# Decoder layer on one core: the filter network's operands first in the DMA queues, its matmuls ahead of the first projections, and the first right taps behind the first filter's sums

## What is computed

```python
res = u @ w_in.T + b_in                          # 768 channels: x0, x1, v
res = _depthwise_conv3(res.transpose(0, 2, 1), conv_w, conv_b)
x, v = res.reshape(B, 3, D, L)[:, :-1], res.reshape(B, 3, D, L)[:, -1]
pe = jnp.sin(t * bands * FREQ)                   # (1024, 33), a constant
h = jnp.sin(FREQ * (pe @ w1.T + b1)) @ w2.T + b2 # the filter network, (1024, 2*256)
h = h * exp(-exp(filt_decay) * t) + filt_bias
for n in range(2):                               # irfft(rfft(v) * rfft(h[n]))[..., :L]
    v = circular_free_convolution(v, h[n]) * x[:, n]
```

## Time and profile before

| | |
|---|---|
| three runs | 823.0, 826.23, 826.8 us, median 826.23 |
| profiled execution | 830.26 us, span 828.1 us from the first to the last instruction |
| busy in the span | PE 702.4 us (85%), DVE 643.4 (78%), ACT 382.0 (46%), POOL 372.0 (45%) |
| mean granted TensorE clock | 0.951 |

### The profile page before, as it was taken

One profiled execution on the slowest core, in us unless ns is written; L12 is line 12 of the kernel. 1 busy time (PEld: TensorE's weight loads), 2 busy tenths in 40 slices (PEclk: granted clock), 3 DMA queues, 4 the chain that ended last, 5 costly groups with the idle time before them and its releaser, 6 DMA issues. The chain is left out here.

```text
span 828.1 us, 12514 instructions
## 1 busy us (share of the span) xinstructions
PE 702.4 (85%) x4398; PEld 507.9 (61%) x4414; DVE 643.4 (78%) x1194; ACT 382.0 (46%) x701; POOL 372.0 (45%) x519
## 2 busy tenths in 40 slices
PE   3889998977989779987798988689999947888893
PEld 1378756866658566576676854477777732555552
DVE  2798778899888998789988751458888826899982
ACT  4432264301473113822126245656666634777773
POOL 0733425653148531485416512707423123476776
PEclk9999999989999899998999999789999996999998
DMA  8250055230052720527410557400000000000012
GB/s 292 80 102 1 0 136 119 51 51 0 7 95 55 179 21 1 102 51 144 73 52 25 137 143 258 149 2 2 2 2 2 2 0 2 1 27 27 33 45 76
DMA packets 37049, 52.79 MB, mean 64 GB/s; under 512 B 4761, under 2 KB 31386, under 8 KB 36732
## 3 DMA queue, kind: packets, MB, share of 16 engines
q0 software_dynamic: 7680, 16.77, 12.7%
q1 hardware_dynamic: 28604, 33.92, 12.3%
q10 hardware_dynamic: 704, 1.32, 0.6%
HBM read 31.04 MB, written 8.39 MB: 48 GB/s over the span
## 5 line engine op out<-in xcount | busy, mean ns | idle before, releaser
L644 ACT ACTIVATE yb<-banks 128x256 f32<-128x256 f32 x64 | 24.4, 385 | 230.2 <-PE banks L407 171.4
L398 PE MATMUL banks<-inv_m,spec_y 128*128 128x256 f32 x384 | 87.6, 381 | 8.0 <-POOL spec_y L765 8.0
L431 PE MATMUL banks<-xt_in,w_in 128*128 128x512 f32 x192 | 86.1, 604 | 3.3 <-DMA xt_in<-in_x_t 3.3
L398 PEld LDWEIGHTS banks<-inv_m,spec_y 128*128 128x128 f32 x384 | 72.3, 190 | 20.7 <-POOL spec_y L765 11.2
L355 PE MATMUL banks<-z_cplx,fwd_m 128*128 128x256 f32 x240 | 73.0, 386 | 10.5 <-DVE prod L989 7.5
L764 POOL TENSOR_TENSOR spec_y<-prod 128x256 f32<-128x256 f32 x64 | 49.2, 769 | 64.1 <-DVE prod L989 63.0
L356 PE MATMUL banks<-z_cplx,fwd_m 128*128 128x256 f32 x240 | 72.3, 383 | 0.0
L431 PEld LDWEIGHTS banks<-xt_in,w_in 128*128 128x128 f32 x192 | 37.0, 194 | 48.6 <-issue 48.4
L369 PE MATMUL banks<-z,fwd_m 128*128 128x256 f32 x168 | 46.0, 436 | 21.0 <-DVE sums_c L936 16.1
L355 PEld LDWEIGHTS banks<-z_cplx,fwd_m 128*128 128x128 f32 x240 | 45.5, 192 | 19.4 <-issue 9.7
L988 DVE TENSOR_TENSOR prod<-banks,spec_h 128x512 f32<-128x512 f32 x64 | 44.0, 687 | 15.5 <-POOL spec_y L765 6.5
(11 more groups left out here) (237 smaller groups left out, 1725.7 us busy)
## 6 DMA issues: line engine op xcount, KB each, us to landing
xt_in<-in_x_t SPq DMA_DIRECT2D x4, 1024.0 KB, 6.6
x_tok<-in_x SPq DMA_DIRECT2D x8, 512.0 KB, 4.3
x_tok<-in_b_out POOLq DMA_DIRECT2D x8, 512.0 KB, 13.2
x_scratch<-x_tok SPq DMA_DIRECT2D x8, 512.0 KB, 2.9
x<-x_scratch SPq DMA_DIRECT2D x8, 512.0 KB, 8.8
v_t<-left POOLq DMA_DIRECT2D x8, 511.5 KB, 5.5
x_t<-left POOLq DMA_DIRECT2D x8, 511.5 KB, 5.0
out<-x SPq DMA_DIRECT2D x7, 512.0 KB, 2.9
```

The source lines that it names most:

```text
L398: last = mm(bank[:, odd * 2 * P:(odd + 1) * 2 * P], spec_y[:, j + odd, part * D + h * P:part * D + (h + 1) * P], inv_m[:, o:o + 2 * P], st ...
L431: last = mm(proj_pair(b, t)[:, c * 512:(c + 1) * 512], w_in[:, k, TILES[t] * P:(TILES[t] + 1) * P], xt_in[:, k, c * 512:(c + 1) * 512], st ...
```

## The change

SP issues `w2` and `b2` directly behind `pe_t` and `w1`, and then `xt_in`. The two loads of `b1` go to ACT's queue, behind `filt_decay` and `neg_t`, with a semaphore of their own, so that PE's first matmuls wait for two transfers and not for four. ACT issues `filt_bias` ahead of `w_in`, and the three small loads of the convolution behind it. PE runs the eight tiles of L470 ahead of the projections of `v`. DVE runs the eight decay products and its two bias adds ahead of the six small operations, and the right taps of `v` behind `filter_sums(0)`, ahead of those of `x0`.

```diff
@@ -213,7 +213,7 @@
         I_0, I_2, I_1, I_5 = range(4)
         QUARTERS = (0, 2, 1, 3)
 
-        ld_net = sem("ld_net"); ld_w2 = sem("ld_w2"); ld_rate = sem("ld_rate"); ld_bias = sem("ld_bias")
+        ld_net = sem("ld_net"); ld_b1 = sem("ld_b1"); ld_w2 = sem("ld_w2"); ld_rate = sem("ld_rate"); ld_bias = sem("ld_bias")
         ld_w_in = sem("ld_w_in"); ld_conv = sem("ld_conv"); ld_ident = sem("ld_ident"); ld_w_out = sem("ld_w_out")
         ld_fwd = sem("ld_fwd"); ld_inv = sem("ld_inv")
         ld_xt = sem("ld_xt"); ld_xtok = [sem(f"ld_xtok{g}") for g in range(2)]; st_x1 = sem("st_x1")
@@ -288,13 +288,11 @@
                         sp.wait_ge(st_x1, 16 * (i + 1))
                         load_group(b + 1, g)
 
-            for dst, src in ((pe_t, d["c_pe"]), (w1, d["w1_t"]), (b1[0:HID], d["b1"]), (b1[HID:P], d["b1"])):
+            for dst, src in ((pe_t, d["c_pe"]), (w1, d["w1_t"])):
                 sp.dma_start(dst, src).then_inc(ld_net, 16)
-            load_xt(0)
             for dst, src in ((w2[0:HID], d["w2_t"]), (w2[HID:HID + 1], d["b2"])):
                 sp.dma_start(dst, src).then_inc(ld_w2, 16)
-            for dst, src in ((b_in[:], d["b_in"]), (conv_w[:], d["conv_w"]), (conv_b[:], d["conv_b"])):
-                sp.dma_start(dst, src).then_inc(ld_conv, 16)
+            load_xt(0)
             sp.dma_start(fwd_m[:], d["c_fwd"].rearrange("p (k c) -> p k c", c=P)).then_inc(ld_fwd, 16)
             sp.dma_start(ident[:], d["c_ident"]).then_inc(ld_ident, 16)
             sp.dma_start(inv_m[:], d["c_inv"]).then_inc(ld_inv, 16)
@@ -453,14 +451,10 @@
                     last.then_inc(out_mm, 1)
 
 
-            pe.wait_ge(ld_net, 16 * 4)
+            pe.wait_ge(ld_net, 16 * 2)
             for c in range(2):
                 last = mm(IB[0][c * HID:(c + 1) * HID, :], w1, pe_t[:, c * 512:(c + 1) * 512], start=True, stop=True)
             last.then_inc(hid_mm, 1)
-            pe.wait_ge(ld_w_in, 16)
-            pe.wait_ge(ld_xt, 16)
-            for t in range(T_X1):
-                project_tile(0, t)
             pe.wait_ge(ld_w2, 16 * 2)
             for i in range(L // P):
                 if i % 4 == 0:
@@ -468,6 +462,10 @@
                 if i >= 4:
                     pe.wait_ge(h_used, i - 3)
                 mm(IB[i % 4][:, :], hid[:, i * P:(i + 1) * P], w2, start=True, stop=True).then_inc(h_mm, 1)
+            pe.wait_ge(ld_w_in, 16)
+            pe.wait_ge(ld_xt, 16)
+            for t in range(T_X1):
+                project_tile(0, t)
             for t in range(T_X0, T_ALL):
                 pe.wait_ge(h_used, 6 + 2 * (t - T_X0))
                 project_tile(0, t)
@@ -583,8 +581,12 @@
 
             act.dma_start(decay_rate, d["filt_decay"].broadcast_to([P, 2 * D])).then_inc(ld_rate, 16)
             act.dma_start(neg_t, d["c_negt"]).then_inc(ld_rate, 16)
+            for dst in (b1[0:HID], b1[HID:P]):
+                act.dma_start(dst, d["b1"]).then_inc(ld_b1, 16)
+            act.dma_start(filt_bias, d["filt_bias"].broadcast_to([P, 2 * D])).then_inc(ld_bias, 16)
             act.dma_start(w_in[:], d["w_in_t"].rearrange("(t p) n -> p t n", p=P)).then_inc(ld_w_in, 16)
-            act.dma_start(filt_bias, d["filt_bias"].broadcast_to([P, 2 * D])).then_inc(ld_bias, 16)
+            for dst, src in ((b_in[:], d["b_in"]), (conv_w[:], d["conv_w"]), (conv_b[:], d["conv_b"])):
+                act.dma_start(dst, src).then_inc(ld_conv, 16)
             act.wait_ge(ld_rate, 16 * 2)
             fn(decay_rate, decay_rate, ACT.Exp).then_inc(act_seq, 1)
             act.wait_ge(act_seq, 1)
@@ -875,7 +877,7 @@
 
             nc.vector.memset(hid[HID:HID + 1, :], 1.0).then_inc(hid_ready, 1)
 
-            dve.wait_ge(ld_net, 16 * 4)
+            dve.wait_ge(ld_b1, 16 * 2)
             dve.wait_ge(hid_mm, 1)
             ts(arg, IB[0], b1, FREQ, ALU.add, ALU.mult).then_inc(vec_seq, 1)
             dve.wait_ge(vec_seq, seq.tick())
@@ -888,6 +890,15 @@
                 dve.wait_ge(vec_seq, seq.tick())
             ts(arg, arg, PI_CLAMP, -PI_CLAMP, ALU.min, ALU.max).then_inc(sin_arg, 1)
 
+            for i in range(L // P):
+                dve.wait_ge(h_mm, i + 1)
+                dve.wait_ge(decay_ready, i + 1)
+                tt(h_time[:, i, :], IB[i % 4][:, :], decay[:, i, :], ALU.mult).then_inc(h_used, 1)
+            dve.wait_ge(ld_bias, 16)
+            for i in range(POOL_BIASED, L // P):
+                dve.wait_ge(h_used, i + 1)
+                tt(h_time[:, i, :], h_time[:, i, :], filt_bias, ALU.add).then_inc(taps_last, 1)
+
             dve.wait_ge(ld_conv, 16 * 3)
             tt(b_mid[:], conv_w[:, :, 2], b_in[:], ALU.mult).then_inc(bias_seq, 1)
             dve.wait_ge(bias_seq, 1)
@@ -898,15 +909,6 @@
             tt(b_end[:], conv_b[:], prod[:, 0, 0:6], ALU.add).then_inc(bias_seq, 1)
             tt(b_mid[:], b_mid[:], prod[:, 0, 0:6], ALU.add).then_inc(bias_seq, 1)
             tt(b_left[:], b_in[:], conv_w[:, :, 0], ALU.mult).then_inc(bias_seq, 1)
-
-            for i in range(L // P):
-                dve.wait_ge(h_mm, i + 1)
-                dve.wait_ge(decay_ready, i + 1)
-                tt(h_time[:, i, :], IB[i % 4][:, :], decay[:, i, :], ALU.mult).then_inc(h_used, 1)
-            dve.wait_ge(ld_bias, 16)
-            for i in range(POOL_BIASED, L // P):
-                dve.wait_ge(h_used, i + 1)
-                tt(h_time[:, i, :], h_time[:, i, :], filt_bias, ALU.add).then_inc(taps_last, 1)
 
             def quarter_sums(x0, x1, x2, x2_copy, x3_copy, s, evacuated=None):
 
@@ -1066,12 +1068,10 @@
                                        ALU.mult, ALU.add, accum_out=row_sum[:, g, t:t + 1])
                         last.then_inc(out_used, 1)
 
-            for t in range(T_V, T_X1):
-                right_tap(0, t)
             dve.wait_ge(taps_ready, POOL_BIASED)
             dve.wait_ge(taps_last, L // P - POOL_BIASED)
             filter_sums(0)
-            for t in range(T_X0, T_ALL):
+            for t in (*range(T_V, T_X1), *range(T_X0, T_ALL)):
                 right_tap(0, t)
             filter_sums(1)
             turned_sums(0)
```

## The result

Nine runs of the changed kernel have a median of 830.18 us (829.47 to 832.04), nine of the kernel before 826.25 (823.0 to 829.04): ratio 1.005, 95% interval 1.003 to 1.0069. The forecast was 828.0 us and no change. The measured 3.9 us lie just inside the 4.1 us that the prediction called no change, the time lies inside its range, and the shift is twice the 1.8 us that the sum had. The profiled execution took 830.65 us with a span of 828.7 us. The span before was 828.1 us, but of an execution 4 us above its kernel's median; so the two spans can't be set against each other, and what moved is read from the start of the program.

The account below looks back on a forecast made before the run. Start of TensorE's step q = 2 taken as the bound: 42.9 + 6.9 + 1.75 + 1.75 = 53.3 us against 51.46, so 1.8 us added to the median 826.23 gives 828.0 us; range 822.5 to 832.0.

Parts of the forecast that it names:

- The rule that decides: TensorE's prologue: the change is worth what it moves the start of step q = 2 (51.46 us), passed on one for one.
- A: Whole prologue: right tap's place, small operations, GpSimd's pass and slow restart eat the earlier taps; 828.0 us, 825 to 831; chance 0.56.
- B: TensorE before q = 0: clock does not fall in the gap, ScalarE's evacuation binds; 825.9 us, no change; chance 0.26.
- C: Prologue: neither clock nor first work slow, VectorE's sums take 9.6 us; q = 2 at 45.3, 820.0 us; chance 0.07.
- D: Sine's argument: b1 lands late, with xt_in at 14.87 us; 5.2 us more, 833.2 us; chance 0.11.
- The right tap is late next: TensorE's step q = 0 waits for v's right tap, now behind VectorE's sums: 42.9 us against 40.32.
- T: End of VectorE's first right tap of v, when step q = 0 can start; forecast 42.9 us.
- GpSimd's pass and the small operations: VectorE's first filter: small operations 1.0, sums 9.6, GpSimd's first pass of real sums 3.8 us; end at 41.7.
- The evacuation chain: From right tap via GpSimd's left-tap DMA to ScalarE's first evacuation: 6.5 us, ending 49.5, hidden by the slow clock.
- The issues on ScalarE: ScalarE's start: five added load issues, 0.6 us each, end at 5.6 us; the sine can start at 13.9.
- The eight products: TensorE's second network product: 7.03 us plus 2.2 as first long work, from 14.7 to 23.9 us.
- The slow restart: TensorE's step q = 0 after a 4.9 us gap runs at a lowered clock: 2.5 us more, bounds 0 and 2.8.

Follow-up runs that it names:

- e4: Changed kernel with eight unused TensorE products of 128 rows added between the network's first and second product; 827.85 us.
- e2: Changed kernel with the two right taps of v put back ahead of the first filter's sums; 828.16 us.
- e3: Changed kernel with the three small loads (b_in, conv_w, conv_b) issued by SyncE behind xt_in instead of by ScalarE; 829.19 us.
- e5: Changed kernel with eight unused TensorE products of 65 rows added between the network's first and second product; +9.5 us against the kernel before (one run).
- e8: e7 with the operands of the network's eight second products padded with zeros from 65 to 128 rows; 823.34 us.
- e10: e8 with VectorE's six small operations put back ahead of the decay products; 817.81 us.
- e7: Changed kernel with e2's and e3's edits together, no products added; 824.54 us.

## Why the prediction was nearly right, and where its size was off

The direction and the place were right: the gain is lost between the taps and q = 2, behind the right tap. That the time came out inside the range and as no change is in part luck: the shift of q = 2 was 5.2 us and not 1.8, two terms of the sum were too small by 6.5 us together, two too large by 3.9, and only 3.9 us of the shift show in the time.

- **The rule that decides** held: the taps arrive earlier, and the gain is lost before q = 2, which moved to 56.65 us and passed on (+5.08 at the first inverse, +3.9 in time). The time is A's, 830.2 in 825 to 831, but not all of A came: three of its four causes did, the slow restart did not. In that one point B was right, the clock stayed up in the gap and ScalarE's evacuation bound TensorE; yet the gap was 2.40 us, not the 4.9 that B was about, and e4's of 5.32 did cost. C and D were not: `b1` landed by 7.51 us, not late.
- **The right tap is late next** held. T was forecast at 42.9 us and was 47.9; e2 shows that the place of the taps costs 3.4 us by itself.
- **GpSimd's pass and the small operations** held closely: from 31.00 + 1.28 = 32.3 us to 46.64 is 14.4 us, and the sum had 1.0 + 9.6 + 3.8 = 14.4. The split was different: part of GpSimd's pass fell on the small operations.
- **The evacuation chain** held: from the tap's end 47.9 to 54.17 + 0.59 = 54.76 us, 6.9 us against 6.5, and it bound TensorE by 0.47 us.
- **The issues on ScalarE** were too cheap. I priced five at 0.6 us each and had the table load at 5.6 us; it came at 7.32, and the sine at 15.59 instead of 13.9. e3 measured the three small ones at 3.1 us in place of my 1.8. The activation did follow its table load after 1.29 us (15.59 - 14.30). So the 830.7 us that the prediction names for a drain behind each load (828.0 and 2.8 are 830.8) is near the measured time by accident.
- **The eight products** are the term that was sized most wrongly. "They last 7.03 us in a running engine", and for the first long work "2.2 us more", so 9.2; they took 13.99. I took the cost of the first long work from the projections, which have 128 rows. In this chain the first long work has 65. With 65 rows the rise did not come in 27.7 us (e5), with 128 it did (e4, e8). That is 4.8 us of the chain. With the 1.7 of the issues, less 1.4 because the last bias adds were shorter (1.28 us instead of 2.64), it makes 5.1, against the 5.0 us by which T was off.
- **The slow restart** ahead of q = 0 was forecast at 2.5 us and did not come: the projections ended 7.7 us later than I had them, so the gap was 2.40 and not 4.9 us, and L367 took its 4.55 us. This error had the other sign. Where the gap is 5.32 us (e4) the cost is 2.3 us, about as priced.

The errors: +4.8 and +1.7, -1.4 (bias adds), -2.5 (restart), +0.5 (evacuation): +3.1, against 56.65 - 53.3 = 3.35 us measured. The rest are starts of a tenth or two each, as the 0.18 us from the tap's end to L367. The low end of the range, 822.5, is 0.7 us below what its three terms give (2.2 + 0.5 + 2.1 = 4.8 below 828.0).

What stays open: why the difference in time departs from the prologue's by up to 1.6 us, and whether the clock's falls further on explain all of it; no run isolated that. In the two profiled executions the prologue differs by 5.1 us and the span by only 0.6: behind the prologue the execution before was 4.5 us slower, and its mean granted clock was 0.951 against 0.959.

## What to carry to other kernels

When a chain is moved ahead, list every wait that its last link's consumer has, and look which of them stands behind the moved work in its own engine's order: here the network was early, and TensorE waited for a right tap that had nothing to do with it. A transfer's issue is work of the engine that issues it: on an engine that is on the chain, even the issue of a 3 KB load took 0.7 to 0.8 us and that of a 9 KB load 1.5. And the work at the start of a program should use as many rows as there are, because here its own speed and that of what followed depended on it; zero rows did as well (e8, e10).

## What the runs showed of the hardware that was not expected

- Products that use 65 of the 128 rows did not raise TensorE's clock from rest: 27.7 us of them ran at 1.7 us each (e5, one execution), and the eight of the changed kernel, e2, e3 and e7 took 13.99 us every time. Padded with zero rows, the same eight took 8.84 and 9.98 us (e8, e10). Once it is up, 65 rows keep it up for at least their 7.03 us.
- The clock column does not show this. For the stretch after in which each product took twice its time, and for one at full speed, it reads 1.00 alike:

```profile
16.30:23.30 7.00, 6.93 (x8) 1.00 1.03 374
...
34.00:46.00 12.00, 11.67 (x28) 1.00 0.00 1
```

  Eight records in 6.93 us are 0.87 us each, two to a product, which is twice the 0.43 of the earlier trace rows. That this is the lower level, 1.2 GHz, is read from the durations; at the start of a program I would believe them and not the column.
- VectorE's operations of 6 columns with both operands in SBUF waited up to 1.0 us for GpSimd, much as those of 512 columns do (1.76 us for what takes 0.68). The Trainium skill, SBUF — State Buffer, section Who interferes with whom, says that a VectorE instruction with two SBUF inputs contends with a GpSimd instruction that reads SBUF, and calls the contention an exclusive lock. The trace agrees, whatever the size: L907 ends at 32.60 + 1.12 = 33.72 us, where GpSimd's first real sum ends at 32.43 + 1.27 = 33.70.
